# Attention scores less their maxima, as pairs of matmuls over one half of the partitions each

## What is computed

```
q = rope(rms_norm(x @ Wq.T));  k = rope(rms_norm(context @ Wk.T));  v = context @ Wv.T
attn = softmax(einsum('bhtd,bhsd->bhts', q, k) * scale)
x = layernorm(x + einsum('bhts,bhsd->bhtd', attn, v) @ Wo.T)
```

## Time and profile before

| | us |
|---|---|
| median of 3 runs | 1313.85 |
| lowest and highest run | 1309.25, 1318.02 |
| profiled execution: span from first to last instruction | 1322.8 |

### The profile page before, as it was taken

How to read it: one execution, slowest core, us unless ns; L and a number is a source line. 1 busy time by engine, 2 the same in 40 slices (tenths; PEclk the granted TensorE clock), 3 DMA queues, 4 the chain that set the end, 5 groups by cost and what they waited for, 6 DMA issues and landing times. The chain is left out here.

```text
span 1322.8 us, 22903 instructions
## 1 busy us (share of the span) xinstructions
PE 1157.0 (87%) x6434; PEld 889.3 (67%) x6466; DVE 1083.4 (82%) x2447; ACT 868.5 (66%) x1581; POOL 579.1 (44%) x1142
## 2 busy tenths in 40 slices
PE   1547999999999999989999999989999999998784
PEld 1436777777777777767777777767777777776551
DVE  3678898988888999888888898888888898886333
ACT  0434667877677777777677666766776667776444
POOL 4244455444445455543445455444444455444200
PEclk6877899988888989988888899988888899898775
DMA  6000001111100111110100111111101111100000
GB/s 198 16 21 3 21 23 29 29 29 29 29 20 15 31 30 29 30 29 29 29 26 8 31 30 29 29 29 29 29 4 30 31 29 29 28 14 11 11 9 17
DMA packets 83117, 37.07 MB, mean 28 GB/s; under 512 B 54837, under 2 KB 82485, under 8 KB 82997
## 3 DMA queue, kind: packets, MB, share of 16 engines
q1 hardware_dynamic: 82997, 35.56, 10.1%
HBM read 24.62 MB, written 8.39 MB: 25 GB/s over the span
## 5 line engine op out<-in xcount | busy, mean ns | idle before, releaser
L499 POOL TENSOR_TENSOR mneg<-zeros,mv 128x2 f32<-128x2 f32 x96 | 18.7, 195 | 445.3 <-DVE mv L1076 445.3
L895 PE MATMUL pb<-q_t,k_blk 128*128 128x256 f32 (+1 forms) x640 | 181.0, 386 | 1.9 <-ACT p_t L692 1.5
L906 PEld LDWEIGHTS pb<-v_blk,p_t 128*128 128x128 f32 (+1 forms) x1280 | 160.3, 208 | 16.2 <-ACT p_t L692 10.8
L906 PE MATMUL pb<-v_blk,p_t 128*128 128x34 f32 (+2 forms) x1280 | 163.9, 292 | 7.1 <-ACT p_t L692 7.1
L666 ACT ACTIVATE gate_silu<-pg,gate_scale 128x512 f32<-128x512 f32 x128 | 88.1, 689 | 103.6 <-PE pu L941 103.6
L697 ACT ACTIVATE hid_int<-hid,magic_p,hid_scale 128x1024 f32<-128x1024 f32 x64 | 78.9, 1236 | 103.4 <-DVE hid_scale L1230 103.4
L1268 DVE TENSOR_REDUCE m_pad<-pb 128x4 bf16<-128x308 f32 x256 | 113.5, 465 | 19.6 <-PE pb L876 19.6
L895 PEld LDWEIGHTS pb<-q_t,k_blk 128*128 128x128 f32 (+1 forms) x640 | 98.7, 188 | 43.7 <-ACT p_t L692 8.3
L1084 DVE SCALAR_TENSOR_TENSOR mix<-dx,vec,x_t 128x256 f32<-128x256 f32 x192 | 117.9, 666 | 6.9 <-POOL dx L562 6.9
L692 ACT ACTIVATE p_t<-pb 128x512 f32<-128x512 f32 (+1 forms) x160 | 95.0, 595 | 40.9 <-PE pb L896 40.0
L711 ACT ACTIVATE x<-raw,nmean,rstd 128x256 f32<-128x256 f32 x128 | 69.9, 593 | 55.5 <-POOL nmean L507 55.0
(11 more groups left out here) (174 smaller groups left out, 3056.0 us busy)
## 6 DMA issues: line engine op xcount, KB each, us to landing
x_t<-xt SPq DMA_DIRECT2D x32, 256.0 KB, 2.8
x_tok<-x SPq DMA_DIRECT2D x32, 256.0 KB, 3.2
out<-outb SPq DMA_DIRECT2D x32, 256.0 KB, 3.2
ctx_t<-ctxt SPq DMA_DIRECT2D x32, 77.0 KB, 3.0
w_sb<-wts SPq DMA_DIRECT2D x8, 256.0 KB, 4.5
v_blk<-v_sb SPq DMA_DIRECT2D x128, 9.6 KB
hid<-wg SPq DMA_DIRECT2D x1, 1024.0 KB, 7.3
hid_int<-wu SPq DMA_DIRECT2D x1, 1024.0 KB, 9.5
```

The source lines that it names most:

```text
L895: mm(dst, k_blk[p][:, g, cols], q_t[p][:, g, :], start=True, stop=False)
L906: last = mm(pb[j][:, c0:c0 + NHEAD[n] * VW], p_t[0:k, q, s, j * P:(j + 1) * P], v_blk[p][0:k, g, n, 0:NHEAD[n] * VW], start=q == 0 and s == 0,
```

## The change

`PAIRS` is regrouped: ((0,0),(0,1)), ((0,3),(0,4)), ((1,0),(1,1)), ((1,3),(1,4)), ((0,2),(1,2)). The eight outer chunks contract over only the 64 partitions on which their heads lie. `shifted_halves(b, p, g)` makes two bank-fuls for one group: for s = 0 and 1 it issues the key matmul of the chunk of the lower half (partitions 0 to 63, into `pb0`), that of the upper half (partitions 64 to 127, into `pb1`), then the two matmuls of the maxima in the same way. `shifted_middle` makes the two middle chunks over all 128 partitions as before, into `pb0`. To fit, maxima of heads 0 to 3 of a group go to partitions g*4 + h and those of heads 4 to 7 to 64 + g*4 + h, the last chunk is padded with 24 zero columns (640 in all), and the exponentials take 128 partitions always. `attend` takes the chunks in the new order, with 104 rows of the last.

```diff
-PAIRS = [((0, 0), (0, 1)), ((0, 2), (0, 3)), ((1, 0), (1, 1)), ((1, 2), (1, 3)), ((0, 4), (1, 4))]
+PAIRS = [((0, 0), (0, 1)), ((0, 3), (0, 4)), ((1, 0), (1, 1)), ((1, 3), (1, 4)), ((0, 2), (1, 2))]
...
+                    pool.memset(k_blk[p][:, :, FLAT:FLATP], 0.0)
...
-                k = ROWS[PAIRS[q][0][1]]
-                sc.activation(flat(p_t[0:k, q, :, :]), pb[q % 2][0:k, :], ACT.Exp).then_inc(pt_ready, 1)
+                sc.activation(flat(p_t[:, q, :, :]), pb[q % 2][:, :], ACT.Exp).then_inc(pt_ready, 1)
...
-            def shifted(b, p, q):
-
-                if q == 0:
-                    pe.wait_ge(mts_ready, b + 1)
-                if q >= 2:
-                    pe.wait_ge(pt_ready, 5 * b + q - 1)
...
+            def shifted_halves(b, p, g):
+
+                if g == 0:
+                    pe.wait_ge(mts_ready, b + 1)
+                else:
+                    pe.wait_ge(pt_ready, 5 * b + 2)
+                for s in range(2):
+                    for half in range(2):
+                        q = 2 * g + half
+                        n, rows = PAIRS[q][s][1], slice(half * HALF, (half + 1) * HALF)
+                        mm(pb[half][:, s * T:(s + 1) * T], k_blk[p][rows, g, n * P:(n + 1) * P], q_t[p][rows, g, :],
+                           start=True, stop=False)
+                    for half in range(2):
+                        q = 2 * g + half
+                        n, rows = PAIRS[q][s][1], slice(half * HALF, (half + 1) * HALF)
+                        last = mm(pb[half][:, s * T:(s + 1) * T], neg_ind[rows, g, n * P:(n + 1) * P], m_t[rows, :],
+                                  start=False, stop=True)
+                        if s == 1:
+                            last.then_inc(st_ready, 1)
+
+            def shifted_middle(b, p):
+                pe.wait_ge(pt_ready, 5 * b + 3)
...
-                if s[3]: shifted(s[3][0], s[3][1], 2)
-                if s[3]: shifted(s[3][0], s[3][1], 3)
-                if s[3]: shifted(s[3][0], s[3][1], 4)
+                if s[3]: shifted_halves(s[3][0], s[3][1], 1)
                 if s[0]: rwkv_in(s[0][0], 0, 1)
+                if s[3]: shifted_middle(s[3][0], s[3][1])
...
-                if s[2]: shifted(s[2][0], s[2][1], 0)
-                if s[2]: shifted(s[2][0], s[2][1], 1)
+                if s[2]: shifted_halves(s[2][0], s[2][1], 0)
```

More of the change, by code:

```diff
@@ L21 @@
 VW = DH + 1
-PAIRS = [((0, 0), (0, 1)), ((0, 2), (0, 3)), ((1, 0), (1, 1)), ((1, 2), (1, 3)), ((0, 4), (1, 4))]
+HALF = P // 2
+HH = HG // 2
+FLATP = NCH * P
+PAIRS = [((0, 0), (0, 1)), ((0, 3), (0, 4)), ((1, 0), (1, 1)), ((1, 3), (1, 4)), ((0, 2), (1, 2))]
 NEG_INF = -1e38
@@ L69, in build @@
         head_mask = sb("head_mask", [P, HG])
-        neg_ind = sb("neg_ind", [P, G, FLAT], bf16)
+        neg_ind = sb("neg_ind", [P, G, FLATP], bf16)
         ones_blk = sb("ones_blk", [P, NCH, 3])
@@ L143, in build @@
         kr = sb("kr", [S, C])
-        k_blk = [sb(f"k_blk{i}", [P, G, FLAT]) for i in range(2)]
+        k_blk = [sb(f"k_blk{i}", [P, G, FLATP]) for i in range(2)]
         v_blk = [sb(f"v_blk{i}", [P, G, NCH, 3 * VW]) for i in range(2)]
@@ L439, in matrices @@
                                        base=0, pattern=[[-1, P]], channel_multiplier=1)
[L440 to L443, removed]
+                for half in range(2):
+                    ind = neg_ind[:, :, half * HH * S:(half + 1) * HH * S].rearrange("p g (h s) -> p g h s", h=HH)
+                    last = pool.affine_select(out=ind, in_=ind, compare_op=ALU.not_equal, fill=-1.0, base=-HALF * half,
+                                              pattern=[[-HH, G], [-1, HH], [0, S]], channel_multiplier=1)
+                last.then_inc(pool_setup, 1)
                 pool.wait_ge(pool_setup, 2)
@@ L884, in maxima_transpose @@
                 last.then_inc(mt_ready, 1)
-            def shifted(b, p, q):
-                if q == 0:
+            def shifted_halves(b, p, g):
+                if g == 0:
                     pe.wait_ge(mts_ready, b + 1)
-                if q >= 2:
-                    pe.wait_ge(pt_ready, 5 * b + q - 1)
[L892 to L896, removed]
+                else:
[6 more added lines that the diff above has]
+                           start=True, stop=False)
+                    for half in range(2):
+                        q = 2 * g + half
[6 more added lines that the diff above has]
+                pe.wait_ge(pt_ready, 5 * b + 3)
+                for s, (g, n) in enumerate(PAIRS[4]):
+                    dst = pb[0][:, s * T:(s + 1) * T]
+                    mm(dst, k_blk[p][:, g, n * P:(n + 1) * P], q_t[p][:, g, :], start=True, stop=False)
+                    last = mm(dst, neg_ind[:, g, n * P:(n + 1) * P], m_t[:, :], start=False, stop=True)
                 last.then_inc(st_ready, 1)
@@ L1266, in maxima @@
                 dve.wait_ge(sc_ready, 8 * b + n + 1)
-                h0 = g * HG + part * 4
-                v.tensor_reduce(out=m_pad[:, j, h0:h0 + 4],
+                c0 = part * HALF + g * HH
+                v.tensor_reduce(out=m_pad[:, j, c0:c0 + HH],
                                 in_=pb[1 - n % 2][:, 0:4 * S].rearrange("p (h s) -> p h s", s=S),
```

## The result

The changed kernel is slower: 1337.66 us median (1331.95 to 1340.46) against 1312.76 (1309.25 to 1318.02), ratio 1.0174 with the interval 1.0134 to 1.0214. A second measurement gave 1.0172. The forecast was 1312.0 with a range up to 1335. The profiled executions differ by 14.6 us, 1337.4 less the 1322.8 of the earlier trace rows, and the medians by 24.9: the profiled execution of before was slower than each of the timed runs of its kernel. So this pair of profiles shows less of the loss than there is.

What follows compares the result with a forecast made beforehand. Bound taken: the circle of VectorE's part and TensorE's answer to `qr`, not TensorE's work. Sum: 0 in ordinary steps, -1.9 us over five restarts, 1322.8 to 1320.9 profiled; off 1313.85, 1312.0 us; range 1294 to 1335.

Steps and rivals of the forecast that it cites:

- What bounds the kernel: Whole step: a circle through VectorE and TensorE sets its 37.5 us; TensorE work beside VectorE's part has 1.37 us to spare.
- The circle of `qr`: Ordinary step: VectorE works from `raw` to `qr`, 29.8 us; TensorE answers from `qr` to `raw`, 7.68 us.
- The outer chunks: Groups 0 and 1 on TensorE: 1.3 us a group instead of 2.17, saving 0.87 each, 1.74 a step.
- Going over to the halves: Switches between whole and half array, four times a step: 0.1 us each taken, between nothing and 0.27.
- My upper bound: Array switches: at most 0.27 us each, from 0.70 us records of a first matmul that nothing precedes against 0.43.
- The wait for the exponentials: Ahead of group 1: idle 1.65 us until 666.95 for exponential 1; `attend` starts 0.9 us late, `raw` unchanged, 0 us.
- The 0.45 us that I left to the transposes: Ordinary step, behind `attend`: what remains of TensorE's 1.37 us wait for `qr` once `attend` ends at 675.75.
- the signs of being wrong that the prediction gave: No `qr` wait in ordinary steps, a group far from 1.3 us, clock 0.50 between 665 and 671, or VectorE's part changed.
- the one of the clock: Sign of failure: granted clock 0.50 between 665 and 671 us of an ordinary step.
- Where the loop starts again: Restart steps, one in four: group 0 ends 0.8 us sooner, `attend` ends ahead of `qr`, 0.38 us saved five times, 1.9 us.
- the clock, counted at 0: Ahead of group 1: the new 1.65 us idle does not lower the clock, as at the loop restart; 0 us.
- The first rival: Shifted scores: clock falls behind the 1.65 us idle, 1.25 us in each of about 28 steps, 35 us, 1347; chance 0.12.

## Why the prediction was wrong

**What bounds the kernel: right.** The circle of `qr`, TensorE's answer and VectorE's part holds in the changed kernel: 37.4 us a step (898.0 / 24), 7.65 us from `qr` to `raw`, 1.74 us less work a step by the forecast and no gain. (The 37.5 us of the prediction are a mean with a restart step in it; the ordinary step of the earlier trace rows took 37.3.)

**The outer chunks: mis-sized, no matter.** 1.3 us a group was forecast; it is 1.08, full overlap. Going over to the halves costs the 0.1 us of the first pair. The way out is 0.29 us behind group 0 (665.19 plus 0.11 to 665.59) and 0.09 behind group 1 (669.28 to 669.37), and the projection's records span 1.13 us where they spanned 1.03. So the 0.1 that I took was right for most switches and low for one. My upper bound rested on a misread row: the 0.70 at 665.96 does not stand where nothing precedes, it follows the projection directly, and from its start to the next matmul it costs 0.54. The Trainium skill's rule that a change of mode drains the array (TensorEngine Tiling (Array Packing), Key Properties) is in keeping with a cost on the way out; that it is a drain, these rows don't show.

**The wait for the exponentials: right in size.** 668.09 is 50 ns behind the end of exponential 1, the bare waits are 1.37 and 0.69 us, `attend` is 0.97 us late where 0.9 was forecast. The 0.45 us that I left to the transposes were not there: `attend` takes 4.99 us, since its end now runs at half clock, and they follow it directly. I had allowed for this slow end in the restart step and forgot it in the ordinary ones. It cost nothing that shows: `raw` still comes 7.65 us after `qr`. Of the signs of being wrong that the prediction gave, the first did come, no wait for `qr`; the one of the clock did not, in this step it is up in the shifted scores:

```profile
668.00:672.00 4.00, 3.50 (x22) 2.36 (x22) 3.96 (x7) 1.93 (x6) 3.84 (x8) 1.00 0.08 8
```

**Where the loop starts again: wrong.** I let the 1.65 us run from the end of group 0, so that 0.8 us arrived. The changed kernel:

```profile
742.61 1.13 PE L830 MATMUL pk<-mix,w_sb 128*128 128x256 f32 x4 [2.33 <-issue]
```

The idle time is 2.33 us: most of what group 0 gave up became idle time. The 1.9 us of gain did not come.

**The step that failed: the clock, counted at 0.** I took one step and multiplied it. The idle time of 1.65 us that I worked out (1.37 measured) was harmless in the loop, as the restart row had said. But the last steps have no key projection between the groups, and the wait there is 2.62 us, longer than anything that my evidence covered. The first rival named the mechanism and its place, group 1; it put it in all 28 steps at 1.25 us, and it came in three, at 3 to 5 us each in the first profile. My rule for when it decides, the 0.45 us to spare, said nothing on how long a wait brings the clock down. And the row that I leaned on, 740.00 to 741.60 at 1.00, shows the clock during an idle time and not behind it. The run that shows the step to be the wrong one is the one with 8 unread matmuls in the long wait: 1.3 of the 1.7% went.

**What adds up, and what stays open.** With the last three elements put right the kernel is 0.3% slower, with the new form in these alone 0.6%; together they are 1.7%. The profiles show why the sum fails: the last three steps take 121.0 us in the second of these kernels and 127.8 in the changed one. 4.4 of these 6.8 us are in the first of the steps, 36.9 us (1161.0 to 1197.9) against 41.3 (1170.5 to 1211.8): there the wait is 1.73 us and the clock stays up, in the changed kernel it is 2.62 and the clock falls. So the last steps cost about 1.4 of the 1.7%, what putting them right gave back. What stays open is what decides whether the clock falls behind such a wait. Its length alone does not, since 2.11 us went either way, and which part the half-height matmuls have in it isn't separated either. The 0.3% outside the last steps isn't located: 894.3 and 898.0 us in the loop stand against 895.4 and 891.9 before and 888.5 in the run with the new form at the end only, within what single executions differ by.

## What to carry to other kernels

Look at the first and last steps of a pipeline by themselves: the work that covers a wait in the middle is missing there. Before work is taken from TensorE, ask what will stand in its place; if it is idle time, the next matmuls may pay double. And where a trace shows part of the chain at the lower clock, a few unread matmuls there are worth a try: in the kernel before they were worth 2.8%, while the rewritten matmuls never gained anything. It takes measuring, though: in the changed kernel two smaller doses left the time at 1.0201 and 1.0188, no better than none, and the third brought 0.994.

## What was not expected of the hardware

Two 64-row f32 matmuls on the two halves of the array cost together what one over 128 rows costs: 0.54 us with their bf16 partners, for 1.08 one after the other. An idle time of 2.62 us on TensorE was followed by the 1.2 GHz level and one of 1.37 us in the step shown was not; one of 2.11 us was in one execution and wasn't in another of the same program. 1.9 us of unread matmuls in the first kept 2.4 GHz. The idle time at the loop's restart, in which nothing is waited for, is no constant: 1.65 us before, 2.33 after, 2.1 to 2.3 with 9 more matmuls a step in the changed kernel, 4.8 to 5.95 with 13 more, and 1.55 with 7 more in the kernel before. What sets it was not tried.
